# A perceiver layer in one fp32 kernel: FFN weights quantised in the key/value phase, value/output product moved into the loop, bias vectors from row sums

## The reference

```python
# 1. cross attention, 16 x 64 queries of 512, 16 x 512 context tokens, the best 32 scores kept
q = x_norm @ Wq.T + bq; k = ctx @ Wk.T + bk; v = ctx @ Wv.T + bv
scores = einsum('btd,bsd->bts', q, k) / sqrt(512)      # top_k 32, others -inf
x = x + softmax(scores) @ v @ Wo.T + bo
# 2. wave attention, 16 heads of 32, per batch of 64 tokens, on x_norm
q, k, v, gate = split(x_norm @ Wqkvg.T + bqkvg)
deposit = (elu(k) + 1) * v                              # per token
conv = causal convolution of deposit over tokens with a damped cosine per head
wave = (elu(q) + 1) * (softmax(coupling) @ conv) * sigmoid(gate)
x = x + wave @ Wout.T + bout
# 3. FFN, 512 -> 2048 -> 512, with ternary weights
tern(w) = clip(round(w / max(mean|w|, 1e-8)), -1, 1)
x = x + gelu(x_norm @ tern(W1).T + b1) @ tern(W2).T + b2
```

## Time and profile before

| | |
|---|---|
| median of 3 runs | 502.63 us (502.43 to 503.21) |
| span of the profiled execution | 499.2 us |
| mean granted TensorE clock | 0.969 |
| PE, DVE, ACT, POOL busy | 93%, 66%, 49%, 48% |
| moved by transfers | 40.5 MB, mean 81 GB/s |
| chain that ended last | PE 50%, DVE 27%, ACT 8%, POOL 5%, issue 5%, DMA 3% |

### The profile page before, as it was taken

How to read it: one execution, slowest core, us unless ns; L and a number is a source line. 1 busy time by engine, 2 the same in 40 slices (tenths; PEclk the granted TensorE clock), 3 DMA queues, 4 the chain that set the end, 5 groups by cost and what they waited for, 6 DMA issues and landing times.

```text
span 499.2 us, 6243 instructions
## 1 busy us (share of the span) xinstructions
PE 462.3 (93%) x2172; PEld 365.9 (73%) x2172; DVE 328.8 (66%) x585; ACT 242.2 (49%) x385; POOL 239.9 (48%) x267
## 2 busy tenths in 40 slices
PE   6949999868999999989959999999998999999996
PEld 2436875647888887768748888888786888888885
DVE  0859999869799999995476579464675323252333
ACT  1258983847678787765423444643345111121211
POOL 2530909567689777782260068133433673323230
PEclk9978999979899999999989999999999999999999
DMA  6994072052344333243000030000000000020002
GB/s 230 402 405 166 0 252 86 6 164 85 105 149 135 120 119 136 84 164 131 1 0 1 1 106 1 21 1 0 1 1 0 1 0 0 1 85 1 1 0 84
DMA packets 19998, 40.54 MB, mean 81 GB/s; under 512 B 1920, under 2 KB 1920, under 8 KB 19456
## 3 DMA queue, kind: packets, MB, share of 16 engines
q1 hardware_dynamic: 19968, 40.16, 22.9%
HBM read 38.05 MB, written 2.10 MB: 80 GB/s over the span
## 4 chain that ended last, share of the span: by engine, by line
PE 50%; DVE 27%; ACT 8%; POOL 5%; issue 5%; DMA 3%; SPq 1%; DVEq 0%; ACTq 0%
PE bank L1460 6%; PE bank L1461 5%; PE bank L1476 5%; PE bank L1474 5%; PE bank L1099 5%; PE bank L1101 5%; PE bank L1100 5%; POOL nat_lo L377 3%; PE bank L1152 3%; DMA ctxr<-ctx 2%; PE bank L1246 2%; DVE mt_lo L898 2%; DVE ln_s L737 2%; DVE xn L999 2%; PE bank L1106 2%
## 5 line engine op out<-in xcount | busy, mean ns | idle before, releaser
L377 POOL TENSOR_TENSOR nat_lo<-ctxr,nat_hi 128x512 fp32r<-128x512 f32 x64 | 83.8, 1336 | 20.1 <-ACT nat_hi L571 19.7
L712 ACT ACTIVATE g<-bank,b1c 128x512 f32<-128x512 f32 x32 | 22.1, 690 | 88.9 <-PE bank L1476 88.9
L1079 DVE CAST g_hi<-g 128x512 fp32r<-128x512 f32 x32 | 13.7, 427 | 74.6 <-ACT g L712 74.5
L1460 PE MATMUL bank<-w2s,g_lo 128*128 128x512 f32 x128 | 50.0, 390 | 1.8 <-DVE g_lo L1081 1.8
L439 POOL TENSOR_SCALAR w2s<-w2t 128x512 fp32r<-128x512 int8 x32 | 19.8, 620 | 66.0 <-PE bank L1461 66.0
L1474 PE MATMUL bank<-xt_lo,w1s 128*128 128x512 f32 x128 | 50.0, 391 | 0.0
L1476 PE MATMUL bank<-xt_hi,w1s 128*128 128x512 f32 x128 | 49.8, 389 | 0.0
L1461 PE MATMUL bank<-w2s,g_hi 128*128 128x512 f32 x128 | 49.8, 389 | 0.0
L549 ACT ACTIVATE mt_hi<-bank 128x512 fp32r<-128x512 f32 x64 | 37.5, 596 | 20.8 <-PE bank L1246 20.5
L898 DVE TENSOR_TENSOR mt_lo<-bank,mt_hi 128x512 fp32r<-128x512 f32 x64 | 43.4, 683 | 6.1 <-ACT mt_hi L549 5.8
L1246 PE MATMUL bank<-ident,ctxr 128*128 128x128 f32 x256 | 40.5, 285 | 6.6 <-DMA ctxr<-ctx 6.5
(11 more groups left out here) (232 smaller groups left out, 1217.0 us busy)
## 6 DMA issues: line engine op xcount, KB each, us to landing
ctxr<-ctx SPq DMA_DIRECT2D x32, 512.0 KB, 3.5
w1raw<-w1T SPq DMA_DIRECT2D x1, 4096.0 KB, 21.9
w2raw<-w2T SPq DMA_DIRECT2D x1, 4096.0 KB, 29.4
wgraw<-wgT SPq DMA_DIRECT2D x4, 1024.0 KB, 5.1
resid<-x SPq DMA_DIRECT2D x2, 1024.0 KB, 9.0
out<-resid SPq DMA_DIRECT2D x8, 256.0 KB, 2.2
wqraw<-wq SPq DMA_DIRECT2D x4, 256.0 KB, 3.7
wkraw<-wk SPq DMA_DIRECT2D x4, 256.0 KB, 4.8
```

What stands on the lines that cost most here:

```text
L377: pool.tensor_tensor(nat_lo[:, par, c, :], ctxr[:, b % 4, c, :], f(nat_hi[:, par, c, :]), ALU.subtract).then_inc(nat_lo_ok, 1)
L1460: pe.matmul(to, g_lo[:, n % 2, token(k)], w2s[:, n % 2, :], start=(c == 0), stop=False)
```

## The change

1. *FFN weights.* They are no longer loaded in the opening. A staging tile `wst` of four slots of 1 MB takes 1 MB chunks in the key/value phase: chunks 0 to 7 for the absolute sums (ScalarE, one pass per chunk, in the ring, between relu and `dep_hi`), chunks 8 to 15 the same weights a second time for the ternary passes. The first half of a ternary pass (scale and upper clip, `clip_part`) goes to GpSimd, the second (lower clip, to int8, `ternary`) stays on VectorE. Chunks 10 to 15 share two slots, each loaded when the ternary pass two before is done. All conversion of convolution results (`conv` lies over the same memory) waits for the last ternary pass.
2. *Context* tiles 0 to 3 are loaded in the opening right away.
3. *Bias vectors* come from row sums on VectorE (`row_sum`) and one small product each.
4. *Value/output product.* Its sixteen fp32 matmuls go between chunks and scores: parts 0 to 2 into iteration 1, part 3 into iteration 2. The per-token constants of tiles 4 to 7, the mixing matrix and the norms of the convolution kernel go into iteration 0.
5. The order of the opening changes: M1's last step behind four transposes, q products by token half first, exp and sine of the kernel table between q parts on ScalarE.

```diff
@@ SP: opening, then the streams @@
+            for n, a in enumerate((freq, damp, phase)):
+                sp.dma_start(wpar[:, n, :], a.partition_broadcast(P)).then_inc(par_in, 16)
+            sp.dma_start(cpl[0:H, :], coup).then_inc(par_in, 16)
             for o in range(DC):
                 sp.dma_start(wqraw[:, o, :], rows(wq)[:, o, :]).then_inc(wqk_in[o], 16)
                 sp.dma_start(wkraw[:, o, :], rows(wk)[:, o, :]).then_inc(wqk_in[o], 16)
+                sp.dma_start(resid[:, 2 * o:2 * o + 2, :], x_v[:, 2 * o:2 * o + 2, :]).then_inc(x_in[o], 16)
-            sp.dma_start(w1raw[:, :, :], rows(w1T)).then_inc(w1_in, 16)
-            sp.dma_start(w2raw[:, :, :], rows(w2T)).then_inc(w2_in, 16)
             for b in range(B):
-                if b < 4:
-                    sp.wait_ge(tern_ok, b + 1)
...
-            sp.wait_ge(v_ps, NT)
-            sp.dma_start(woutraw[:, :, :], rows(woutT)).then_inc(wout_in, 16)
-            sp.dma_start(bias_o[:, :], bout.partition_broadcast(P)).then_inc(bout_in, 16)
+            for k in (0, 1, 2, 3, 4, 5, 8, 9, 6, 7):
+                if k < 4:
+                    sp.wait_ge(wg_lo_ok[k], 1)
+                elif k < 6:
+                    sp.wait_ge(abs_ok, k - 3)
+                elif k < 8:
+                    sp.wait_ge(abs_ok, k - 1)
+                else:
+                    sp.wait_ge(abs_ok, k - 5)
+                sp.dma_start(w_stage(k), w_chunk(k)).then_inc(wst_in[w_slot(k)], 16)
+            for k in range(10, 16):
+                sp.wait_ge(tern_ok, k - 9)
+                if k == 12:
+                    sp.wait_ge(v_ps, NT)
+                    sp.dma_start(woutraw[:, :, :], rows(woutT)).then_inc(wout_in, 16)
+                    sp.dma_start(bias_o[:, :], bout.partition_broadcast(P)).then_inc(bout_in, 16)
+                sp.dma_start(w_stage(k), w_chunk(k)).then_inc(wst_in[w_slot(k)], 16)
@@ GpSimd: behind split_lo(2), split_lo(3) @@
+            def clip_part(k):
+                n, c = k // 4, k + 8
+                pool.wait_ge(scale_ok, n + 1)
+                pool.wait_ge(wst_in[w_slot(c)], w_landed(c))
+                v = wst[:, w_slot(c), :]
+                pool.tensor_scalar(v, v, winv[:, n + 2:n + 3], 1.0, ALU.mult, ALU.min).then_inc(clip_ok, 1)
@@ ScalarE: key/value ring, and before the convolution copies @@
                     act.activation(k_raw[:, t, :], k_raw[:, t, :], ACT.Relu).then_inc(kact_ok, 1)
+                    for k in ((), (0,), (1,), (2, 3), (4,), (5,), (6,), (7,))[t]:
+                        abs_part(k)
...
-            act.wait_ge(wg_lo_ok[2], 1)
-            act.wait_ge(wg_lo_ok[3], 1)
+            act.wait_ge(tern_ok, 8)
@@ VectorE: row sums, key/value ring, q features @@
+            def sums_part(o):
+                dve.wait_ge(wqk_in[o], 32)
+                link(row_sum(sum_k, wkraw, 0, o))
+                row_sum(sum_q, wqraw, 1, o).then_inc(sums_ok, 1)
...
                 dve.tensor_tensor(feat, feat, v_raw[:, t, :], ALU.mult).then_inc(dep_ok, 1)
+                if t == 5:
+                    scale_of(0, bank[7][:, 0:4])
+                if t >= 6:
+                    ternary(t - 6)
...
             for n in range(2 * DC):
                 q_feature(n)
+                if n < 2:
+                    ternary(n + 2)
+                elif n == 2:
+                    scale_of(1, bank[0][:, 0:4])
+                elif n < 7:
+                    ternary(n + 1)
@@ TensorE: totals @@
                 v_product(t)
+                if t == 4:
+                    total(bank[7][:, 0:4], 0)
...
                 features(bank[4 + n % 4][:, :], wgq_hi, wgq_lo, n).then_inc(wq_ps, 1)
+                if n == 0:
+                    pe.wait_ge(kb_ok, NT - 1)
+                    total(bank[0][:, 0:4], 1)
```

More of the change, by code:

```diff
@@ L418, in _ @@
             pool.wait_ge(toe_zero, 4)
+            for k in range(4, 8):
+                clip_part(k)
             pool.wait_ge(bout_in, 16)
@@ new lines, in first_xt, with row_sum @@
+            def first_xt(ts):
+                for t in ts:
+                    xt_lo_part(t, t, turn_bank(t))
+            def row_sum(to, raw, col, o):
+                scale = cols[:, col, o:o + 1]
+                if o == 0:
+                    return dve.tensor_scalar(to[:, :], raw[:, o, :], scale, None, ALU.mult)
+                return dve.scalar_tensor_tensor(out=to[:, :], in0=raw[:, o, :], scalar=scale, in1=to[:, :],
+                                                op0=ALU.mult, op1=ALU.add)
@@ L764, in _ @@
             link(dve.scalar_tensor_tensor(out=a, in0=q, scalar=2.0, in1=a, op0=ALU.mult, op1=ALU.add))
+            dve.wait_ge(xbias_ps, 1)
+            dve.wait_ge(bo_in, 16)
+            dve.tensor_tensor(bias_x[:, :], bias_x[:, :], bank[4][:, :], ALU.add).then_inc(xbias_ok, 1)
+            dve.wait_ge(tpos_ok, 4)
+            dve.tensor_tensor(tdec[:, :, :], bc(a, CT), tpos[:, :].unsqueeze(1).to_broadcast([P, H, CT]),
+                              ALU.mult).then_inc(dec_ok, 1)
+            dve.wait_ge(turns_ok, 1)
+            for part in (PI_HI, PI_MID, PI_LO):
+                link(dve.scalar_tensor_tensor(out=targ[:, :, :], in0=turns[:, :, :], scalar=-part,
+                                              in1=targ[:, :, :], op0=ALU.mult, op1=ALU.add))
+            absolute(targ[:, :, :], targ[:, :, :]).then_inc(arg_ok, 1)
             dve.wait_ge(cexp_ok, 1)
@@ L806, in _ @@
-            first_xt((4, 5, 6, 7))
-            dve.wait_ge(u_ps, 1)
-            dve.tensor_copy(bqbk[:, :], bank[3][:, 0:1]).then_inc(bqbk_ok, 1)
-            dve.wait_ge(turns_ok, 1)
-            for part in (PI_HI, PI_MID, PI_LO):
-                link(dve.scalar_tensor_tensor(out=targ[:, :, :], in0=tdec[:, :, :], scalar=-part,
-                                              in1=targ[:, :, :], op0=ALU.mult, op1=ALU.add))
-            absolute(targ[:, :, :], targ[:, :, :]).then_inc(arg_ok, 1)
@@ new lines, in _, with coupling @@
+            turn_first(7)
+            q_product(1)
+            q_product(2)
+            pe.wait_ge(sumx_ok, 1)
+            pe.wait_ge(qbias_ok, 1)
+            pe.matmul(bank[4][:, :], ones[:, :].to_broadcast([P, P]), sum_k[:, :], start=True,
+                      stop=True).then_inc(xbias_ps, 1)
+            for n in range(3, 2 * DC):
+                q_product(n)
+            def coupling():
+                pe.wait_ge(cpr_ok, 2)
+                pe.wait_ge(xbias_ok, 1)
+                pe.matmul(bank[4][:, 0:H], cpr[0:H, :], ident[0:H, 0:H], start=True, stop=True).then_inc(coup_ps, 1)
```

503 lines of the change are left out of this document (276 added, 227 removed).

## The result

The changed kernel takes 547.65 us (median of 4 runs, 546.76 to 555.94), the kernel before beside it 502.92 (4 runs): ratio 1.091, 95% interval 1.086 to 1.097. The run of 555.94 is a slow one, and the ratio goes by the fast runs alone. The prediction had the sign and the place right and the size wrong: 513, range to 522. The profiled execution of the change spans 545.0 us.

The account below looks back on a forecast made before the run. TensorE, busy 93% of the span, was taken as the bound. Opening -24.0 plus key/value phase and weight stream +34.2 gave +10.2 on 499.2, 509.4; with a 3.4 offset 512.8, rounded to 513 us, range 505 to 522.

Parts of the forecast that it names:

- Second stream of the weights: Chunks 10 to 15 through two slots, GpSimd clip 2.1 us each; last ternary pass 345.6, first `cvt_lo` 34.2 us later.
- The port rival: Port shared by GpSimd and VectorE: clips hold VectorE's two-input passes, +6 to +9 us, 519 to 522; chance 14%.
- clips or `xn` passes above 3 us: Sign in the new profile that would show clips holding VectorE's two-input passes through the shared port.
- slower clips: Upper bound of the key/value and weight-stream loss, +40 us, together with the upper end of GpSimd's output-bias additions.
- Opening, -24.0: Opening through iteration 2: shorter by 24.0 us, bounds -18 and -29; first `mt_lo` of the loop at 53.6 instead of 85.44.
- after 84: Sign in the new profile: iteration 2 starting after 84 us, instead of the walked 80, would show a thinner opening gain.
- rival 3: Opening gives less: VectorE's small operations or value/output products leave -17 instead of -24 us, 520; chance 10%.
- Iteration 2's idle: TensorE's 4.34 us wait for a context transfer before iteration 2 goes, and with it the half clock, worth 3.0 us.
- Ring, 7.2 us a turn: Key/value phase: abs pass between relu and `dep_hi` makes a turn 7.2 us, 9.3 with two passes, instead of 5.11.
- the wait before the second total: Key/value phase: TensorE waits 7 to 10 us for the eighth abs pass before the second total.
- Rest of the tail: Key/value phase to first `cvt_lo`: +34.2 us, at 357.0 against 322.81, with a TensorE wait of about 9 us.
- Behind it the program is unchanged, so the loss stays: After the first `cvt_lo`: program unchanged and TensorE-bound, so the 34.2 us loss was to carry through to the end.

Follow-up runs that it names:

- c3: Changed kernel with the GpSimd clip's second operation turned from min with 1.0 to add of 0.0: 519.76 us, ratio 1.037 to the kernel before.
- p1: Changed kernel plus measurements behind its last store: clip forms on GpSimd alone, then the clip beside VectorE passes; kernel time not compared, clip 7.58 us.
- q1: Kernel before with one unused tile of 32 bytes ahead of the large regions, nothing else: 505.38 us, ratio 1.008.
- w6: Reworked twelve-chunk version of the change (501.73 us), with GpSimd's output-bias additions made to wait for the seventh ternary pass: 499.49 us, ratio 0.997 to the kernel before.
- c1: Changed kernel with the clip on VectorE, right ahead of each ternary pass, instead of on GpSimd: 523.48 us, ratio 1.044 to the kernel before.
- o1: Changed kernel with GpSimd's eight attention-bias additions moved behind the second `split_q`: 555.34 us, ratio 1.106 to the kernel before.

## Why the prediction was wrong

- **The clip, 2.1 us in "Second stream of the weights"**: the step that failed. It took the rate of a multiply-and-add pass for a multiply-and-min pass; measured 7.78. Worth 28 of the miss of 35 us (c3). With the clip at its assumed price the kernel takes 519.8: inside the range, 7 above the forecast. The port rival was no substitute: its 6 to 9 us were a hold by clips of 2.1 us. Its sign, "clips or `xn` passes above 3 us", did appear, but p1 shows the clip at 7.16 us beside VectorE passes that it does not meet, so the sign could not tell a held clip from a slow one. The tail grew by 62.2 us, and the bound for "slower clips" was +40.
- **Opening, -24.0**: measured -19.8 at the first key add, inside its bounds. What was short are the `targ` passes, which I costed at their old rate though the change puts GpSimd's additions beside them. The 5 us stayed down to iteration 2, which begins at 85.41 instead of 80. By the prediction's own sign ("after 84") that is rival 3; it came beside the clip and cost 4 us. Iteration 2's idle went as said, the value/output products did hide, and the clock was 1.00 from 71 to 99. But the low clock had only moved ahead: TensorE idled 5.46 us up to 59.5, now for VectorE, a wait that I had not walked, and the mean from 58 to 85 was 0.87.
- **Ring, 7.2 us a turn**: right. 6.99, and 8.89 with two passes (9.3 walked); the wait before the second total was 7.60 us (7 to 10 expected), after 3.92 before the first, which was not walked.
- **Rest of the tail**: in c3 the stretch from the first key add (227.6) to `cvt_lo` (338.9) grew by 35.5 us, against +34.2. The walk was good, given its price: c3's last ternary pass ends at 325.9, which with the opening's 19.4 added is 345.3, for 345.6 walked, and TensorE's wait for it was 9.17 us, for 9; a wait of 3.90 before it, for a `toe` pair, was not walked. One step does not follow from its words: chunk 12 was to take three transfer times, 15.3 us at 5.1 each, but the walk left 8.4 behind the third ternary pass. c3 took 9.7.
- **"Behind it the program is unchanged, so the loss stays"**: the instructions are, but they took 3.4 us longer, of which q1 reproduces 2.6 by the addresses alone.
- Added up in c3's profile, the misses are 4.6 (opening, -19.4 there) + 1.3 (tail) + 3.4 (behind it) = 9.3 us above the +10.2 of the sum: 499.2 + 10.2 + 9.3 = 518.7, c3's span. By the medians of c3 and of the kernel before beside it, 519.76 and 501.84, the difference is 17.9 instead of 19.5.

## What to carry to other kernels

Price an instruction from a row with the same pair of operations, not only the same engine and shape; where there is none, take the upper bound at least from the slowest row of that engine. Even that would have fallen short here: a 128x2048 subtraction took 4.97 us, the clip 7.16 or more. Only timing the instruction by itself gives its price. An engine's idle share says whether a pass has room, the instruction issued behind it says whether this place has: moving eight passes behind one small copy gave back 10 us. And compare the parts that a change does not touch: 6 ns per matmul there pointed at tile addresses. Before reading a shift of a few us in one profile, look how far the stretch ahead of the edit moved too (w6).

## What the runs showed of the hardware

- GpSimd, 128x2048 fp32 in place: multiply and min 7.2 to 8.2 us, 7.16 with no waiting (p1, beside passes from PSUM), multiply alone 6.29 with up to 1 us of waiting in it, multiply and add 1.9 to 2.3, min and max 1.90 (p1). Multiply and min on VectorE is 1.28 (c1), the multiplication on ScalarE 2.0 (c2).
- Beside a clip of 7 to 8 us a VectorE pass with one SBUF operand can take 7.5 to 8.2 us instead of 0.7 to 1.2, until the clip ends; one with two took 4.9 to 5.5 instead of 0.69 to 1.22 and was through 1.5 to 2.0 us before the clip's end; one with an operand in PSUM keeps its 0.69 (p1, the changed kernel, o1). With VectorE's pass in first, the clip takes 8.2 instead of 7.16.
- An unused tile of 32 bytes ahead of the large ones cost 0.8%, with 6 ns more on each of the up product's matmuls of 389 ns (q1).
